# 86 products whose results nobody reads on the matrix engine, and a new hand-written order of all queues

## The chip, the cores and the metric

The kernel runs on one core of one Trainium2 chip. A core has a matrix engine (TensorE, PE in the profile), a vector engine (VectorE, DVE), a scalar engine for activations (ScalarE, ACT), GpSimd (POOL), and SyncE (SP), whose queue issues most of the DMA transfers. Each engine works through its own list of instructions in order, and they meet only through semaphores. The metric is the device time of one execution in microseconds.

## The reference

A small transformer on x of shape (8, 256, 128): four residual layers after one another, each behind a layer norm, and the first and last pair of them share the weights of the feed-forward layer.

```
x = x + attn_a(layernorm(x), Wq, Wk, Wv, Wo)      # 16 heads of 8, rotary, causal over 256 tokens
x = x + ffn(layernorm(x), w_gate, w_up, w_down)   # FP4 quantised, inner width 352
x = x + attn_b(layernorm(x), w_qkv, ln_w, w_proj) # 16 heads of 8, causal within groups of 32 tokens
x = x + ffn(layernorm(x), w_gate, w_up, w_down)

ffn:    h = silu(q(x) @ q(w_gate).T) * (q(x) @ q(w_up).T);  out = q(h) @ q(w_down).T
q(t):   per block of 16: scale = max|t| / 6, t / scale rounded to the grid 0 .5 1 1.5 2 3 4 6, times scale
attn_a: softmax(q k^T * scale + causal mask) v, then @ Wo.T
attn_b: q and k are RMS-normed with weight ln_w before the heads are split
```

## The kernel before

One batch of 256 tokens (two tiles of 128) goes through all four layers without leaving SBUF; the eight batches overlap. A batch has these stages:

- `front1`: layer norm, turn of xn to the contraction side (L788, bank 0 of `fb`), four projections for q, k and their rotated forms (L805, 128x256, fp32), rotary on DVE and POOL, and V (L810), which ACT copies to `Vf`. Q and K are split into three bf16 parts, which SP writes to DRAM (`scr_f`, L732) and reads back stacked (`Qf`, `Kf`, L741).
- `front2`: first scores. For each of 16 heads four bf16 products (L844 to L847) into bank 0 or 1 of `fb` in turn, and a maximum over each row on DVE (L1366). The maxima go back as three extra rows of `Qf` (`nmTf`, L749 on SP).
- `front3`: second scores (L875 to L878), exponential on ACT (L1089), products with V (L887, sixteen for four heads), division, projection (L902), residual.
- `ffn_a` 1 to 3: norm and quantisation; gate and up products (L981, L985); quantisation of h, turn (L997) and down projection (L1003).
- `local` 1 and 2: the attention over groups of 32, in the two banks of `lb`. Its last step, L1455, adds the result to x and raises `l_done`.
- `ffn_b` 1 to 3: the same as `ffn_a`, then the store.

`weights`, once: the FFN weights are quantised and turned (L780, L782).

The order is written out by hand in the table `TIMES`. For each engine and stage it has a line per batch with a number per step, and `weave` (below) issues the steps of an engine by rising number. A step that is early in the list waits on its semaphore and holds up what is behind it on its engine. `FFN_TURNS` says in which order the two FFNs use the two banks of `ffb`; a phase waits for the one before it.

In the first front PE issues the turn, the projections and V, and its next instruction is the first score of batch 0, which needs `Kf` read back from DRAM. At the end it works for the last batch's `ffn_b` alone, with the down projection of batch 6 just ahead.

The last two batches are finer: `SPLIT` has the quantisation of h done tile by tile. x of batches 2 to 7 is loaded by `load` on SP (L755), at the place that `TIMES["sp.load"]` gives.

Of the kernel before, what the change touches and what calls it, by code (L numbers as in the profile page):

```python
# [13 lines left out]
P = 128  # L14
NBATCH, SEQ, D = 8, 256, 128
T = SEQ // P
# [30 lines left out]

SPLIT = {("a", 6), ("a", 7), ("b", 6), ("b", 7)}
# [17 lines left out]
5 9  # L66
11 12
13 15
16 17
19 20  # L70
23 24
# [3 lines left out]
10  # L75
14
18
21
22
27  # L80
30
31""",
    "sp.load": """
0
1
2
3
4
6
7  # L90
8""",
    "sp.store": """
32
33
# [25 lines left out]
380 381 385 386 393 394 404 406 410 411 413 417 418 423 424 428 437""",  # L120
    "pe.front3": """
# [31 lines left out]
316 320 323 325 328
392 396 399 401 402
460 463 464 467 469
505 506 507 509 510""",
    "pe.ffn_b2": """
218 223 224 234 237
271 285 289 299 306
375 377 378 382 383  # L160
442 446 449 451 454
493 495 496 498 499
511 514 515 516 517
532 533 535 536 537
552 553 554 555 556""",
    "pe.ffn_a3": """
114 116 117 118
173 174 176 178
239 240 242 244
307 309 310 312  # L170
364 365 367 370
434 435 438 440
484 487 488 490
520 522 523 525""",
    "pe.ffn_b3": """
333 338 339 350
409 412 425 429
472 473 480 482
501 502 503 504
526 527 528 529  # L180
540 541 542 543
548 549 550 551
557 558 559 560""",
# [4 lines left out]
7 10 13 16  # L188
24 29 32 34
39 48 49 53  # L190
72 79 82 83
107 116 117 123
169 190 193 200
214 224 225 228""",
    "act.front2": """
6
37
69
104
# [1342 lines left out]
```

## Time and profile before

| | |
|---|---|
| median of 3 runs | 408.29 us (407.53 to 409.46) |
| profiled execution | 406.49 us, span 404.6 us |
| PE, DVE, ACT, POOL busy | 78%, 70%, 60%, 37% of the span |
| mean granted clock of TensorE | 0.884 |
| DMA | 17.56 MB, mean 43 GB/s |

A busy share is an average over stages that have different limits. The granted clock is the share of full speed that TensorE was given: it has two levels here, 1.00 (2.4 GHz) and 0.50 (1.2 GHz), and a value between them is a stretch that has both. The first low stretch that a record marks begins at 17.4 us; up to 13.9 us there is no record of the clock, and the page shows 1.00 there. Times in a timeline are from the start of the span. In the chain of waits each piece is the work that the next one waited for.

### The profile page before, as it was taken

How to read it: one execution, taken by the hardware profiler on the slowest of the kernel's cores; microseconds unless marked ns; L12 is line 12 of the kernel's file. 1: busy time of each engine (PE TensorE's matmuls, PEld its weight loads, DVE VectorE, ACT ScalarE, POOL GpSimd, SP SyncE). 2: the span in 40 equal slices, each digit the busy share in tenths (PEclk: the TensorE clock that was granted, in tenths of full speed). 3: DMA queues.
4: the chain of work that ended last, by engine and by line, in shares of the span. 5: the costliest groups of instructions: out<-in, count | busy, mean ns of one | idle time of the engine just before them, and what ended most of it. 6: DMA issues, size and time to landing. Idle time of an engine off the chain costs nothing.

```text
span 404.6 us, 9187 instructions
## 1 busy us (share of the span) xinstructions
PE 315.1 (78%) x3533; PEld 215.4 (53%) x3533; DVE 283.4 (70%) x746; ACT 241.2 (60%) x630; POOL 148.6 (37%) x210
## 2 busy tenths in 40 slices
PE   1408688698798989889798998899989676757654
PEld 0305445365565856565566676568547544535423
DVE  2626406739878899883898599879958889647551
ACT  2211173256488499587836985786898587474431
POOL 6050044131560481334256243613533556150503
PEclk9855679579999999978999999989999998989565
DMA  5570055056024000250150204000100000000000
GB/s 164 145 158 0 4 126 108 4 104 133 6 80 79 4 2 2 56 104 2 41 115 8 66 14 80 5 2 2 29 2 12 6 15 0 2 15 14 2 13 13
DMA packets 33151, 17.56 MB, mean 43 GB/s; under 512 B 1898, under 2 KB 32938, under 8 KB 33108
## 3 DMA queue, kind: packets, MB, share of 16 engines
q1 hardware_dynamic: 32820, 16.85, 18.3%
q8 instruction: 28, 0.46, 0.5%
q10 hardware_dynamic: 288, 0.13, 0.1%
q14 instruction: 15, 0.12, 0.1%
HBM read 9.43 MB, written 7.34 MB: 41 GB/s over the span
## 4 chain that ended last, share of the span: by engine, by line
PE 36%; DVE 29%; ACT 20%; issue 8%; POOL 5%; DMA 1%; SPq 1%; ACTq 0%; DVEq 0%; POOLq 0%
DVE bmax L1366 7%; PE fb L805 5%; PE fb L887 3%; PE ffb L1003 3%; PE ffb L981 3%; PE fb L844 2%; PE fb L875 2%; ACT prob L1089 2%; PE lb L944 2%; ACT Qd L1134 2%; ACT Kd L1132 2%; PE ffb L985 2%; DMA Kf<-scr_f 1%; PE lb L918 1%; PE ffb L997 1%
## 5 line engine op out<-in xcount | busy, mean ns | idle before, releaser
L1366 DVE TENSOR_REDUCE bmax<-fb 128x3 f32<-128x384 f32 x128 | 65.8, 544 | 11.1 <-PE fb L847 10.6
L1089 ACT ACTIVATE prob<-fb 128x384 f32<-128x384 f32 x128 | 59.3, 497 | 19.8 <-PE fb L878 19.4
L844 PE MATMUL fb<-Kf,Qf 50*128 50x256 bf16 x128 | 30.7, 298 | 22.4 <-DMA Kf<-scr_f 14.1
L1265 POOL TENSOR_TENSOR fa__w<-fa__w,fa__c 128x704 f32<-128x704 f32 (+1 forms) x10 | 13.8, 1378 | 56.7 <-DVE fa__w L1509 56.7
L875 PE MATMUL fb<-Qf,Kf 53*128 53x256 bf16 x128 | 29.3, 287 | 5.2 <-ACT prob L1089 4.3
L844 PEld LDWEIGHTS fb<-Kf,Qf 50*128 50x128 bf16 x128 | 10.5, 94 | 37.9 <-DVE bmax L1366 19.7
L887 PE MATMUL fb<-prob,Vf 128*32 128x128 f32 (+1 forms) x512 | 29.0, 346 | 1.3 <-ACT prob L1089 1.1
L1265 POOL TENSOR_TENSOR fb__w<-fb__w,fb__c 128x704 f32<-128x704 f32 (+1 forms) x10 | 13.7, 1374 | 43.5 <-DVE fb__w L1509 43.5
L805 PE MATMUL fb<-xnTf,wT 128*128 128x256 f32 x64 | 23.6, 533 | 2.4 <-ACT xnTf L1017 2.4
L846 PE MATMUL fb<-maskb 64*128 64x128 bf16 x128 | 24.4, 234 | 0.0
L845 PE MATMUL fb<-Kf,Qf 50*128 50x128 bf16 x128 | 24.3, 232 | 0.0
L847 PE MATMUL fb<-maskb 64*128 64x128 bf16 x128 | 24.1, 230 | 0.0
L877 PE MATMUL fb<-maskb 64*128 64x128 bf16 x128 | 23.2, 226 | 0.0
L876 PE MATMUL fb<-Qf,Kf 53*128 53x128 bf16 x128 | 23.0, 223 | 0.0
L878 PE MATMUL fb<-maskb 64*128 64x128 bf16 x128 | 22.8, 221 | 0.0
L875 PEld LDWEIGHTS fb<-Qf,Kf 53*128 53x128 bf16 x128 | 10.0, 93 | 23.6 <-ACT prob L1089 10.2
L1228 POOL TENSOR_TENSOR qk<-ra,rb 128x512 f32<-128x512 f32 x7 | 9.0, 1293 | 34.8 <-DVE rb L1347 34.8
L887 PEld LDWEIGHTS fb<-prob,Vf 128*32 128x32 f32 x512 | 14.2, 113 | 13.2 <-issue 3.2
L1003 PE MATMUL ffb<-wdT,fb__hqT 128*128 128x128 f32 (+1 forms) x96 | 16.9, 326 | 4.7 <-ACT fb__hqT L1017 4.7
L805 PEld LDWEIGHTS fb<-xnTf,wT 128*128 128x128 f32 x64 | 16.4, 269 | 7.7 <-ACT xnTf L1017 4.3
L1346 DVE TENSOR_TENSOR ra<-fb,ropet 128x512 f32<-128x512 f32 x8 | 5.5, 686 | 21.0 <-PE fb L805 20.9
L944 PEld LDWEIGHTS lb<-Kd,Qd 128*128 128x128 f32 x128 | 19.2, 215 | 0.6
(201 smaller groups left out, 942.1 us busy)
## 6 DMA issues: line engine op xcount, KB each, us to landing
scr_f<-partsf SPq DMA_DIRECT2D x16, 192.0 KB, 2.4
Qf<-scr_f SPq DMA_DIRECT2D x16, 192.0 KB, 3.8
Kf<-scr_f SPq DMA_DIRECT2D x16, 192.0 KB, 5.0
scr_f<-partsf SPq DMA_DIRECT2D x16, 128.0 KB, 1.9
xall<-in_L_attn_a_x_dram SPq DMA_DIRECT2D x8, 128.0 KB, 3.1
scr_f<-partsf SPq DMA_DIRECT2D x16, 64.0 KB, 1.6
out_dram<-xall SPq DMA_DIRECT2D x8, 128.0 KB, 1.8
ropet<-in_rope_dram SPq DMA_DIRECT2D x1, 512.0 KB, 3.6
```

Of the source, the lines that this page charges most:

```text
L805: mm = pe.matmul(fb[:, n // 2, (n % 2) * SEQ:(n % 2 + 1) * SEQ], wT[:, n, :], xnTf[:, :], start=True, stop=True)
L844: pe.matmul(S[:, 128:384], Qf[k, g, 128:256], Kf[k, g, 0:256], start=True, stop=True, skip_group_check=True)
L845: pe.matmul(S[:, 0:128], Qf[k, g, 0:128], Kf[k, g, 0:128], start=False, stop=True, skip_group_check=True)
L846: pe.matmul(ends(S, 0, 64), eye_lo[half_, :], twice(m_qk[half_, :]), start=False, stop=True, skip_group_check=True)
L847: mm = pe.matmul(ends(S, 64, 64), eye_hi[half_, :], twice(m_qk[half_, :]), start=False, stop=True, skip_group_check=True)
L875: pe.matmul(S[:, 128:384], Kf[k, g, 0:128], Qf[k, g, 0:256], start=True, stop=True, skip_group_check=True)
L887: mm = pe.matmul(S[32 * j:32 * j + 32, k * P:SEQ], Vfs[b % RING][:, k, h, :], p, start=(k == 0), stop=(k == 1), skip_group_check=True)
L944: mm = pe.matmul(lb[:, t, n * P:(n + 1) * P], Qd[:, w, :, :].rearrange("p j q -> p (j q)"), Kd[:, w, :, :].rearrange("p g k -> p (g k)"), ...
L1003: mm = pe.matmul(ffb[:, t, 0:D], w.hqT[0:k, t, c, :], wdT[0:k, c, :], start=(c == 0), stop=(c == 2))
L1089: act.activation(prob[:, slot % 8, :], S[:, 0:384], ACT.Exp).then_inc(f.s_exp, 1)
L1265: pool.tensor_tensor(w.w[:, cols], w.w[:, cols], w.c[:, cols], ALU.subtract).then_inc(w.s_hdif, t1 - t0)
L1366: dve.tensor_reduce(bmax[:, h, 1:4], fb[:, h % 2, 0:384].rearrange("p (n k) -> p n k", k=P), AX.X, ALU.max).then_inc(bmax_done, 1)
```

## The change

It adds a step function `work` to PE, with 86 matrix products in it. Each multiplies the identity by columns of the projection weights `wT` and writes a bank that nobody reads at that time: bank 0 of `lb` in the first three batches' `work`, before the local attention of batch 0 uses it or between its uses, and bank 3 of `fb` in the last, when all fronts are over. The counts are 28, 10, 8 with 256 columns and 12, 6, 22 with 128. The first product of each group waits for a semaphore: Vf of batch 0 is copied; the shifts of batch 0, and of batch 1, are turned; the last local attention is added; xq of the last batch is turned back; both halves of the last h have their gate. The others of a group wait for nothing.

Beside it, all of `TIMES` is new, for the five engines, and `FFN_TURNS` with it.

```diff
+HEAD_WORK = [28, 10, 8]
+TAIL_WORK = [12, 6, 22]
 FFN_TURNS = [
     ("a", 0, "up"), ("a", 0, "down"), ("a", 1, "up"), ("a", 1, "down"),
-    ("a", 2, "up"), ("b", 0, "up"), ("a", 2, "down"), ("a", 3, "up"),
-    ("b", 1, "up"), ("a", 3, "down"), ("a", 4, "up"), ("b", 0, "down"),
+    ("a", 2, "up"), ("b", 0, "up"), ("a", 2, "down"), ("b", 0, "down"),
+    ("a", 3, "up"), ("b", 1, "up"), ("a", 3, "down"), ("a", 4, "up"),
...
+    "pe.work": """
+3 4 5 6 7 8 9 10 11 12 13 14 15 16 17 18 19 20 21 22 23 24 25 26 27 28 29 30
+50 54 59 60 64 65 70 72 75 82
+106 111 134 139 144 148 149 155
+
+
+594 595 596 597 599 600 601 602 605 606 607 610
+612 614 615 617 619 620
+621 622 623 624 625 626 627 628 629 630 631 632 633 634 635 636 637 638 639 643 644 645""",
...
+            spare = {
+                0: (HEAD_WORK[0], 2, lb[:, 0, :], f.s_v, 1),
+                1: (HEAD_WORK[1], 2, lb[:, 0, :], f_nmT, 1),
+                2: (HEAD_WORK[2], 2, lb[:, 0, :], f_nmT, 2),
+                5: (TAIL_WORK[0], 1, fb[:, 3, :], l.s_done, NBATCH),
+                6: (TAIL_WORK[1], 1, fb[:, 3, :], ffn_b.s_xqT_ready, NBATCH),
+                7: (TAIL_WORK[2], 1, fb[:, 3, :], ffn_b.s_hg, T * NBATCH),
+            }
+
+            def work(b):
+                for n in range(spare[b][0] if b in spare else 0):
+                    yield
+                    _, width, bank, *ready = spare[b]
+                    if n == 0:
+                        pe.wait_ge(*ready)
+                    pe.matmul(bank[:, 0:width * P], identf, wT[:, 0:width, :].rearrange("p n k -> p (n k)"), start=True, stop=True)
+                yield
+
-            passes("pe", weights=weights, front1=front1, ...
+            passes("pe", work=work, weights=weights, front1=front1, ...
```

Line numbers below L46 move by 12 in the changed kernel (the projections are L817, the first scores L856, the added products L1036).

PE at the first front, before: L805 are the projections of batch 0, L810 its V, L844 to L847 the first head's scores.

```order
L805 MATMUL fb<-xnTf,wT 128x256 x4
L810 MATMUL fb<-wT,xnTf 128x128 x2
L844 MATMUL fb<-Kf,Qf 128x256
L845 MATMUL fb<-Kf,Qf 128x128
```

And now:

```order
L817 MATMUL fb<-xnTf,wT 128x256 x4
L822 MATMUL fb<-wT,xnTf 128x128 x2
L1036 MATMUL lb<-wT,identhm 128x256 x28
L856 MATMUL fb<-Kf,Qf 128x256
L857 MATMUL fb<-Kf,Qf 128x128
```

The 28 added products stand where PE had nothing between V and the first score; behind them the sixteen heads and the weights follow as before.

PE at the front of batch 1 in the changed kernel: L864 turns the shifts of batch 0, L800 turns xn, L887 is the first of the second scores.

```order
L864 MATMUL fb<-maskb,npartf 128x128 x2
L800 MATMUL fb<-identhm,xnf 128x128 x2
L1036 MATMUL lb<-wT,identhm 128x256
L817 MATMUL fb<-xnTf,wT 128x256 x4
L887 MATMUL fb<-Qf,Kf 128x256
```

One added product has come between the turn and the projections; it is so once more in the front of batch 3. Nine further ones are spread over the second scores of batch 0 and the front of batch 2.

SP before, from the end of the setup: `scr_f` are the stores of the parts, `xall` the loads of x.

```order
L755 DMA xall<-in_L_attn_a_x_dram 128x2x128 x3
L732 DMA scr_f<-partsf 128x3x256
L732 DMA scr_f<-partsf 384x1x256
L732 DMA scr_f<-partsf 128x2x256 x2
L732 DMA scr_f<-partsf 128x256 x2
L755 DMA xall<-in_L_attn_a_x_dram 128x2x128 x3
L741 DMA Qf<-scr_f 48x8x256 x2
L741 DMA Kf<-scr_f 48x8x256 x2
L749 DMA Qf<-nmTf 3x8x256 x2
```

And now:

```order
L744 DMA scr_f<-partsf 128x3x256
L744 DMA scr_f<-partsf 384x1x256
L744 DMA scr_f<-partsf 128x2x256 x2
L744 DMA scr_f<-partsf 128x256 x2
L753 DMA Qf<-scr_f 48x8x256 x2
L753 DMA Kf<-scr_f 48x8x256 x2
L761 DMA Qf<-nmTf 3x8x256 x2
L767 DMA xall<-in_L_attn_a_x_dram 128x2x128
```

All six loads of x have moved behind the first reads of Qf and Kf, and behind the shifts of batch 0, for which SP waits.

PE at the end in the changed kernel: L997 is the last up product of batch 7, L1009 turns hq, L1015 is the down projection.

```order
L1036 MATMUL fb<-wT,identhm 128x128
L997 MATMUL ffb<-wguT,fb__xqT 128x352
L1036 MATMUL fb<-wT,identhm 128x128 x21
L1009 MATMUL ffb<-identhm,fb__hq 128x128 x3
L1015 MATMUL ffb<-wdT,fb__hqT 128x128 x3
L1009 MATMUL ffb<-identhm,fb__hq 128x128 x3
L1036 MATMUL fb<-wT,identhm 128x128 x3
L1015 MATMUL ffb<-wdT,fb__hqT 128x128 x3
```

Before, the same real products stand there in the same order, with nothing between them. Earlier, eleven of the added ones stand around the down projection of batch 6, and four among the gate and up products ahead of these rows.

## Rows read from the trace of the kernel before

**Rows 1.** The page: busy time by engine, and the clock in 40 slices.

```profile
PE 315.1 (78%) x3533; PEld 215.4 (53%) x3533; DVE 283.4 (70%) x746; ACT 241.2 (60%) x630; POOL 148.6 (37%) x210
...
PEclk9855679579999999978999999989999998989565
```

**Rows 2.** Windows: stretch, its length, busy us per engine, clock, DMA share, GB/s.

```profile
17.40:48.00 30.60, 13.84 (x83) 9.39 (x84) 14.98 (x33) 5.47 (x10) 5.49 (x4) 0.50 0.30 66
...
54.90:61.70 6.80, 6.76 (x43) 4.15 (x42) 0.60 (x2) 3.56 (x8) 1.24 (x3) 0.50 0.75 155
...
72.00:85.60 13.60, 9.81 (x50) 6.00 (x49) 7.67 (x25) 3.00 (x8) 2.25 (x5) 0.50 0.32 53
...
90.00:330.00 240.00, 212.82 (x2748) 147.44 (x2747) 199.05 (x537) 176.58 (x475) 99.06 (x135) 0.98 0.17 37
...
375.70:389.40 13.70, 10.17 (x29) 6.52 (x30) 5.93 (x18) 4.41 (x10) 5.83 (x8) 0.50 0.04 11
...
392.80:404.60 11.80, 4.83 (x18) 3.74 (x18) 2.34 (x6) 2.40 (x5) 3.55 (x4) 0.50 0.04 11
```

**Rows 3.** The chain of waits: start us, us, what.

```profile
24.36 5.29 DMA Kf<-scr_f
...
30.41 1.36 PE ffb L780 x6
...
33.71 0.39 PE fb L844
...
35.08 0.39 PE fb L844
...
56.12 1.44 PE fb L887 x16
...
59.49 3.04 PE fb L805 x8
...
62.92 0.79 PE fb L887 x16
...
80.40 3.78 PE fb L805 x8
...
133.45 1.92 PE fb L805 x8
```

**Rows 4.** Windows before a fall of the clock, or without a rise.

```profile
14.00:17.30 3.30, 0.76 (x5) 0.52 (x4) 3.21 (x5) 0.45 (x2) 0.00 (x0) 1.00 0.56 172
...
33.70:41.30 7.60, 6.63 (x46) 4.45 (x47) 5.53 (x12) 0.01 (x1) 0.00 (x0) 0.50 0.00 0
...
68.60:71.90 3.30, 2.60 (x24) 1.72 (x22) 3.27 (x11) 0.38 (x1) 1.54 (x3) 1.00 0.43 120
```

**Rows 5.** Timeline of the first fronts: start, length, instruction [idle before <-releaser].

```profile
15.58 0.38 ACT L1017 ACTIVATE Vf<-fb 128x256 f32<-128x256 f32 x1 [5.37 <-PE fb L810]
...
21.32 1.46 SPq L755 DMA_DIRECT2D xall<-in_L_attn_a_x_dram  x3
...
45.65 3.17 PE L805 MATMUL fb<-xnTf,wT 128*128 128x256 f32 x8 [0.47 <-ACT xnTf L1017]
```

**Rows 6.** The end: one row of the chain, the others of the timeline.

```profile
137.84 0.86 PE ffb L1003 x6
...
376.88 0.42 DVE L1455 TENSOR_TENSOR xall<-lb,xall 128x256 f32<-128x256 f32 x1 [0.72 <-PE lb L961]
...
382.88 1.65 PE L1003 MATMUL ffb<-wdT,fb__hqT 128*128 128x128 f32 x6 [0.58 <-ACT fb__hqT L1017]
...
383.02 0.62 POOL L1257 TENSOR_TENSOR fb__xq<-fb__xw,fb__xscale 128x256 f32<-128x256 f32 x1
...
386.13 1.54 PE L981 MATMUL ffb<-wguT,fb__xqT 128*128 128x352 f32 x2 [0.47 <-ACT fb__xqT L1017]
...
396.04 0.90 PE L997 MATMUL ffb<-identhm,fb__hq 128*128 128x128 f32 x3 [5.51 <-POOL fb__hq L1272]
...
397.52 1.65 PE L1003 MATMUL ffb<-wdT,fb__hqT 128*128 128x128 f32 x6 [0.58 <-ACT fb__hqT L1017]
```

More of the change, by code:

```diff
@@ L65 @@
     "sp.front1": """
[L66 to L71, printed above, removed]
+0 1
+6 9
+10 13
+15 16
+20 21
+22 24
 25 26
@@ L74 @@
     "sp.front2": """
-10
-14
-18
-21
-22
+2
+11
+18
+19
+23
 27
 30
-31""",
+33""",
     "sp.load": """
-0
-1
-2
 3
 4
-6
+5
 7
-8""",
+8
+12
+14
+17""",
     "sp.store": """
+31
 32
-33
 34
@@ L158 @@
[L158 to L165, printed above, removed]
-    "pe.ffn_a3": """
[L167 to L174, printed above, removed]
-    "pe.ffn_b3": """
[L176 to L183, printed above, removed]
+49 51 56
@@ new lines @@
+76 79 83
+105 107 117
+165 166 170
+214 227 231
+284 290 295
+338 344 349""",
+    "pe.front2": """
[7 rows of a table added]
+416 417 422 426 427 433 436 439 440 444 447 455 459 467 468 472 477""",
+    "pe.front3": """
[7 rows of a table added]
+485 486 488 490 491 494 495 497 499 500 503 504 507 508 510 511 514 515 519 521 523 526 529""",
+    "pe.local1": """
+169 177 190
+235 241 252
+301 304 325
+390 393 403
+458 463 473
+517 520 527
+546 549 554
+574 577 579""",
+    "pe.local2": """
+199 210 216 220 224 230
+261 262 276 278 288 292
+334 341 348 351 356 358
@@ new lines @@
+410 412 419 420 424 429
+479 481 487 489 493 496
+531 534 539 540 543 544
+558 561 566 567 570 571
+582 585 590 591 592 593""",
+    "pe.ffn_a2": """
+110 114 120 124 131
+171 182 186 193 194
+240 242 243 248 249
+326 329 331 336 337
+385 391 392 396 400
+452 456 457 462 464
+509 512 513 516 518
+545 547 548 550 551""",
+    "pe.ffn_b2": """
+255 265 266 273 277
+345 352 357 362 368
+402 408 409 418 432
+482 483 484 492 498
+536 537 538 541 542
+563 564 565 568 569
+578 580 581 583 584
+609 611 613 616 618""",
+    "pe.ffn_a3": """
@@ L184 @@
+160 161 162 164
+218 219 222 225
+282 283 286 289
+373 374 377 378
+442 443 448 449
+501 502 505 506
+530 532 533 535
+557 559 560 562""",
+    "pe.ffn_b3": """
+308 313 316 320
+470 471 475 476
+522 524 525 528
+552 553 555 556
+572 573 575 576
+586 587 588 589
+598 603 604 608
+640 641 642 646""",
     "act.weights": """
@@ L253 @@
-269 280
-313 321
-359 364
-382 385
+38
+71
+105
+154
+192
+255
+299""",
+    "act.front3": """
[7 rows of a table added]
+305 306 308 309 310 313 314 316 317 318 321 323 325 326 328 330 332 334 337 340 345""",
+    "act.local1": """
+74 77 84 88 90 93
+121 126 131 134 135 139
+167 169 174 179 183 190
+231 233 238 242 243 247
+281 285 287 291 292 296
+331 335 338 342 343 346
+357 360 363 367 368 372
+382 386 387 390 391 393""",
+    "act.local2": """
+106 109 116
+144 150 162
+197 201 211
+254 256 259
+302 304 312
+351 353 358
@@ L257 @@
+376 378 381
+396 399 400""",
+    "act.ffn_a1": """
+36 37
+70 73
+114 117
+170 177
+217 224
+262 268
+307 315
+348 355""",
+    "act.ffn_a2": """
+42 45 54
+81 89 94
+129 133 136
+189 191 194
+232 237 241
+278 282 286
+327 329 333
+359 362 365""",
+    "act.ffn_b1": """
+127 132
+171 186
+225 234
+273 280
+320 324
+361 364
+385 388
 403 405""",
     "act.ffn_b2": """
-143 147 156
-195 201 206
-258 259 263
-306 308 320
-353 354 358
-372 375 378
-391 393 395
+140 145 153
+203 210 213
+245 252 258
@@ L266 @@
+301 303 311
+352 354 356
+377 379 380
+392 394 395
 407 408 409""",
     "act.ffn_a3": """
-65 68 70
+65 68 69
 103 111 112
-145 159 160
-192 209 211
-240 253 254
-286 300 301
-337 338 348 349
-373 374 379 381""",
-    "act.ffn_b3": """
-162 235 241
-255 289 292
-303 342 345
-351 362 363
-369 383 384
+143 157 158
+206 220 221
+250 271 272
+297 319 322
+336 339 347 350
+366 371 373 375""",
+    "act.ffn_b3": """
+161 180 181
+230 294 295
+300 341 344
+349 369 370
+374 383 384
 389 397 398
-400 402 404 406
+401 402 404 406
@@ L284 @@
 410 411 412 413""",
     "pool.weights": """
-1 2""",
+2 3""",
     "pool.front1": """
 0
-3 4 5 6
+1 4 5 6
 7 8 9 10
-11 14 15 16
-17 23 24 25
-26 30 32 34
-35 47 49 51
-54 60 61 64""",
+12 14 15 16
+17 23 24 26
+27 32 34 36
+40 44 47 49
+51 54 55 58""",
     "pool.local1": """
-21 27
-31 38
+21 25
+31 37
 43 48
-59 62
-68 73
-78 84
-89 95
-104 106""",
+61 63
+71 74
+80 83
+91 95
+103 105""",
     "pool.ffn_a1": """
-12 13
+11 13
 20 22
-33 36
-42 45
-55 58
-69 71
-79 82
-91 94""",
-    "pool.ffn_b1": """
@@ L315 @@
-37 39
-44 46
-57 66
-72 74
-80 83
-93 96
-103 105
-112 114""",
+30 33
+45 52
+59 60
+68 70
+76 78
+89 92""",
+    "pool.ffn_b1": """
+35 38
+50 53
+62 64
+72 73
+79 88
+93 98
+104 106
+113 114""",
     "pool.ffn_a3": """
@@ L325 @@
 28 29
-40 41
-50 53
-63 65
-75 76
-85 86 87 88
-99 100 101 102""",
-    "pool.ffn_b3": """
-52 56
-67 70
-77 81
-90 92
-97 98
+39 41
+56 57
+65 66
+75 77
+84 85 86 87
+96 97 99 100""",
+    "pool.ffn_b3": """
+42 46
+67 69
+81 82
+90 94
+101 102
 107 108
-109 110 111 113
+109 110 111 112
 115 116 117 118""",
     "dve.weights": """
-4 6 7 9 13 15""",
+4 6 7 9 13 21""",
     "dve.front1": """
@@ new lines @@
+46 49 54
+102 104 109
+167 168 171
+244 245 252
+315 318 324
+384 386 392
+441 444 453
+502 503 506""",
+    "dve.local1": """
+120 122 125 132
+175 179 182 203
+248 249 255 277
+344 346 349 363
+419 420 422 434
+483 484 487 501
+522 528 532 554
+573 575 579 597""",
+    "dve.local2": """
[7 rows of a table added]
+601 602 605 606 607 608 612 614 621""",
+    "dve.ffn_a1": """
[7 rows of a table added]
+508 510 512 513 523 525 526 530""",
+    "dve.ffn_a2": """
+79 81 84 87
+135 139 145 146
+199 200 205 207
+296 297 300 301
+355 360 361 362
+423 426 427 430
```

176 lines of the change are left out of this document (38 added, 138 removed), and 106 rows, old and new, of tables (FFN_TURNS, TIMES).

## The prediction

> **What bounds the kernel now.** I read first the page: busy shares and the slices of the granted clock [rows 1]. PE is the busiest engine (315.1 us, 78%), DVE next, and the clock of TensorE stands at about half in the first fronts and in the last batch. Then the busy time by stretch [rows 2]. From 90 to 330 us the clock is 0.98 and DVE works 199.05 of 240 us, so the middle is a matter of DVE and of the order. Outside it there are five stretches at 0.50, which is the 1.2 GHz level: 30.6 + 6.8 + 13.6 + 13.7 + 11.8 = 76.5 us. PE is busy for only part of them, so the question is how much PE work in them lies on the chain that ended last. That chain was read third [rows 3]. At the low level the four projections of a front (L805) take 3.04 and 3.78 us, at full speed 1.92.
>
> What PE did before the clock fell or stayed low [rows 4]: in 14.0 to 17.3 us it worked 0.76 us, and the clock fell. In 33.7 to 41.3 us it issued nothing but the scores of batch 0, busy for 6.63 of 7.6 us, and the clock stayed at 0.50. In 68.6 to 71.9 us, at full speed, it mostly issued scores of batch 1 (2.60 of 3.3 us) and the clock fell. The first low stretch ended at 48.0 us, when the projections of 45.65 to 48.82 us [rows 5] were nearly over. So dense fp32 products lift the clock and scores alone do not hold it. The added products are of the first kind (f32, 128x128 weights), so I take them to hold it wherever they stand close together.
>
> **The parts, against the profiled execution.** It took 406.49 us (span 404.6 and 1.9 around it), 1.8 us under the median of 408.29 that the runs show. Differences are carried over to the median.
>
> (1) 28 products, 256 columns wide, before the first scores. They begin when Vf of batch 0 is copied (15.58 + 0.38 = 15.96 us, [rows 5]), at full clock. One costs what one product of L805 costs: 1.92 / 4 = 0.48 us at full speed, 3.17 / 4 = 0.79 to 3.78 / 4 = 0.95 at half. 28 x 0.48 = 13.4, to 29.4 us. The last Kf transfer lands at 24.36 + 5.29 = 29.65 [rows 3]. They fit, with 0.3 us to spare; the last one's end is counted in each 0.48, so the room is somewhat larger.
>
> (2) First scores and turned weights. Two pairs of heads and the turns at L780 and L782, from 29.7 to about 33 us, then run at full speed. The turns stand at 1.36 us for the six of L780 [rows 3] and half as much again for L782, 2.0 us in all; half of it less the last one's latency is 0.9. The first scores give 0.4. A pair of heads repeats every 35.08 - 33.71 = 1.37 us: scores 0.39 + 3 x 0.11 and a maximum 0.57; at full speed the scores are an estimated 0.46 (half of 0.72 and 0.1 of latency), so a pair takes 1.10, and 0.27 is saved. Two such pairs: 0.5. Sum -1.8. Bounds: 0 if the clock falls at once, and -1.8 - 4 x 0.27 - 1.27 (projections of batch 1) - 0.35 (the turns ahead of them) = -4.5 if it never falls. I take -1.8, since [rows 4] show scores alone losing the clock.
>
> The page "TensorE: Matmul & The Clock Gate" of the Trainium skill (Part 4, PE-mode transpose) says that transposes do not count as PE activity in the usual way. No run here shows it alone. By it the turns at L780 would not help to hold the clock, and the sum of (2) would be nearer to -0.9.
>
> (3) One product stands between the turn of xn and the projections of batches 1 and 3. There PE waits 0.47 us for ACT before 45.65 [rows 5]. At half speed a product (0.85) reaches 0.4 past it: +0.4 each, +0.8. Bounds 0 and +1.0.
>
> (4) Nine products among the second scores of batch 0 and the projections of batch 2. 54.9 to 61.7 us is at 0.50 and PE is busy 6.76 of 6.8 us [rows 2], so here PE is the bound. Full speed saves 3.04 - 1.92 = 1.1 on L805, 1.44 - 0.79 = 0.65 on the 16 products of L887 [rows 3], and some 0.5 on the scores between: 2.3. Against this the products: of nine, three in the bound part, 3 x 0.44 = 1.3. Net -1.0. Bounds -2.3 (all in gaps) and +2.0 (nine in the chain, 4.3, less 2.3).
>
> (5) 72.0 to 85.6 us. The scores of batch 1 have no product between them; they stand one after another in the new order as before. I expect the clock to fall as it did, and 0. Bounds: -2.3 (1.9 of it L805 at 80.40) and 0. The other seven products stand among outputs of batch 1 and scores of batch 2, where the clock was full anyway; PE has gaps there: +0.2.
>
> (6) SP no longer issues three loads of x (1.46 us, [rows 5]) ahead of the reads of Qf and Kf. The reads wait for the stores' landing, so little is gained: -0.3 (bounds 0 and -1.5). The loads come later, ahead of the next reads; x of batch 2 is asked for at about 46 us, behind the shift rows of batch 0, and needed ahead of the projections at 59.49. If that cover were gone, a load of 128 KB, at most the 5.29 us of a Kf transfer, would show.
>
> (7) The end. The last local attention is added at 376.88 + 0.42 = 377.3 us; four products at the low level follow (narrow ones, half of (1): 0.40 to 0.48), to about 379.2, and may push the turn of hq behind them by about 1 us. The next turn waits for POOL anyway, so this is absorbed if the clock is up by then. After that, at full speed: down projection L1003 1.65 becomes 0.86 [rows 6], which lets batch 7's turn of xq come 1.0 earlier (bound from then on by POOL, done at 383.64). Gate products L981: 1.54 becomes about half, and the second gives about 0.35: 1.1. At the very end a turn of 0.90 and two down projections of 1.65 on the chain become an estimated 0.45, 0.86 and 0.86: 2.0. The 21 products ahead of it need 21 x 0.24 = 5.0 us, and PE sits idle 5.5 us before 396.04. The three between the last turn and last product cover ACT's copy and stick out an estimated 0.2; the four before the first down projection 0.2. Sum -1.0 - 1.1 - 2.0 + 0.4 = -3.7. Bounds: -5.0 and, if all is at half speed, 19 x 0.48 = 9.1 against 5.5: +3.6, and 1 above.
>
> (8) The new order of all engines. From 90 to 330 us DVE idles 41 us. A new order can only move within these: a tenth of it is 4 us either way. On DVE the last batch's first FFN is finished 11 instructions earlier of 649. One takes 283.4 / 746 = 0.38 us, so 4.2 us, but what is pushed behind it must still be done; I count a quarter, -1.0. Bounds -4 and +4.
>
> Sum: -1.8 + 0.8 - 1.0 + 0.2 - 0.3 - 3.7 - 1.0 = -6.8. 406.49 - 6.8 = 399.7; from the median 401.5.
>
> **The rivals.** About 0.5% (2 us) is what a measurement of this kernel can tell from no change.
>
> A, the clock holds through the first scores too, and on into the front of batch 3: another 2.7 from (2), 2.3 from (5) and the 0.8 of (3) back, less 0.4 for lost cover: 396.1. For it: 28 products right ahead, and earlier transfers. Against: [rows 4].
>
> B, the head's gain is eaten before 90 us by DVE and ACT, and the order gives nothing. Then only the end counts, -3.7: 404.6. For it: in 72.0 to 85.6 us PE is busy for only 9.81 of 13.6 us [rows 2], so part of what it does faster ends in waiting. Against: from 55 to 61.7 us PE has no gap. The same page (Part 1, the tip on the warm-up budget) puts the cost of the clock's ramp at under 1% of a typical span; by that rule all of it here would be below 4.0 us, a time of 404.3 or more. The trace speaks against it: 76.5 us at half clock are 19% of the span, though only a part of them lies on the chain.
>
> C, the new order loses in the middle. The order of all five queues changes, and turns of the two FFNs change place. If it costs the 4 us of (8) and head and end bring 4: 408.
>
> D, slower: the added products run at half speed. This is decided at 16 us. Each of the 28 at half speed takes 0.32 to 0.47 us more; from the second on they are later than Kf. All 28 at 0.85: 15.96 + 23.8 = 39.8 against 29.7, +10.1, and the end adds 3.6 at most; with 0.8 for (3) and without gains elsewhere 408.3 + 10.1 = 418 or more; if the clock comes back after some ten of them, +3.5, the end's +1 and no gain: 413. For it: the 0.76 us of work from 14.0 to 17.3 did not hold the clock. Against: it is up at 15.96, and from then on there is no gap.
>
> **Chances.** Forecast 0.45 (own range 398.5 to 404.5), A 0.20, B 0.13, C 0.11, D 0.07, more than A 0.04. Faster by over 0.5% (below 406.3) is forecast, A, B and the rest: 0.82, less 0.02 for their edges: 0.80. C lies half within and half beyond: same 0.10, slower 0.10. The range leaves out D, half of C and what lies beyond A: 394.5 to 407.0.
>
> **What would show it.** (1): the first scores start at 29.3 to 30.0 us; a start at 31 or later speaks for D. (2): the turns of L780 take 0.7 us, and the low clock returns before 37. (4): no low clock between 52 and 64. (5): low clock again from about 70 to 82; if not, A. (7): clock 1.00 from about 380 (old time) to the end, the last down projection 0.86 us long. (8): last batch's first FFN done earlier than the head's gain alone explains. Wrong would be the whole if the clock's level did not change where the products stand, or if the first scores came late.

## The result, and the profile after

The changed kernel took 398.43 us (median of 4 runs, 395.03 to 401.78), the one before 408.88 us beside it: a ratio of 0.971, 95% interval 0.966 to 0.976. The forecast was 401.5 us, range 394.5 to 407.0. The profiled execution took 399.24 us, with a span of 397.3 us. A ratio here is taken from the executions of a kernel that lie within 1.5% of its fastest, a median from all of them, so the two can differ, and of the kept traces e1's (409.45 us) and e8's (456.2 us at a mean clock of 0.651) are not of such executions. Behind the added products the line numbers of the changed kernel are 32 above those of before (L1403 is now L1435).

The page of the kernel after (the rows that answer [rows 1]):

```profile
PE 335.2 (84%) x3705; PEld 240.6 (61%) x3705; DVE 283.4 (71%) x746; ACT 243.3 (61%) x630; POOL 150.6 (38%) x210
...
PEclk9996699599999699899999999999999988986799
```

PE has 20.1 us more work, DVE has exactly what it had. The clock row is full in the first slices and in the last ones. Windows of the kernel after: stretch, its length, busy us of PE, PEld, DVE, ACT and POOL, granted clock, DMA share, GB/s. They answer [rows 2] and [rows 4].

```profile
13.20:33.50 20.30, 17.33 (x104) 13.73 (x102) 14.65 (x24) 5.26 (x9) 5.59 (x4) 1.00 0.42 92
33.70:47.10 13.40, 10.45 (x54) 6.93 (x54) 5.90 (x15) 0.76 (x2) 0.00 (x0) 0.50 0.04 12
47.30:71.00 23.70, 21.58 (x218) 14.11 (x217) 10.04 (x30) 12.31 (x28) 7.21 (x8) 1.00 0.42 95
71.20:81.30 10.10, 6.07 (x29) 4.19 (x28) 6.36 (x21) 2.38 (x6) 3.77 (x7) 0.50 0.25 70
90.00:330.00 240.00, 214.87 (x2748) 151.33 (x2747) 200.59 (x544) 179.91 (x481) 98.49 (x133) 0.97 0.16 36
354.60:364.60 10.00, 8.46 (x24) 5.32 (x23) 3.99 (x7) 5.64 (x15) 3.21 (x3) 0.50 0.00 0
371.60:378.20 6.60, 5.76 (x27) 5.46 (x27) 4.81 (x15) 3.82 (x9) 4.59 (x6) 0.50 0.00 0
378.40:395.30 16.90, 14.55 (x104) 12.45 (x102) 6.94 (x18) 4.96 (x10) 4.89 (x6) 1.00 0.03 9
```

Of the five low stretches of [rows 2] the first is 13.4 us long in place of 30.6, the second is gone, the third 10.1 in place of 13.6, the fourth 6.6 in place of 13.7, and the fifth gone: from 378.4 us to the end the clock is full. The clock first falls among the first scores of batch 0, 5.7 us after the dense products ended. The middle is at 0.97, as good as before. But there is a new low stretch, 10.0 us long, ahead of the last local attention, at 354.6 us; before, the clock was low there for 3.2 us only, from 362.2.

The chain of waits after (start us, us, what), which answers [rows 3]:

```profile
23.52 5.29 DMA Kf<-scr_f
...
29.32 0.76 PE ffb L792 x6
...
42.40 0.85 PE lb L1036 x2
43.26 3.41 PE fb L817 x8
...
78.76 0.85 PE lb L1036 x2
79.62 2.67 PE fb L817 x8
...
393.90 0.86 PE ffb L1015 x6
```

The turns at L792 (L780 before) take 0.76 us in place of 1.36, so the clock was full at 29.3. The added products at 42.40 and 78.76 are on the chain, at half speed, as step (3) has them. Timeline of PE after, first fronts and end (answers [rows 5] and [rows 6]):

```profile
15.62 12.35 PE L1036 MATMUL lb<-wT,identhm 128*128 128x256 f32 x56 [0.47 <-ACT Vf L1049]
...
43.05 3.62 PE L817 MATMUL fb<-xnTf,wT 128*128 128x256 f32 x8
...
59.25 1.99 PE L817 MATMUL fb<-xnTf,wT 128*128 128x256 f32 x8
...
79.41 2.87 PE L817 MATMUL fb<-xnTf,wT 128*128 128x256 f32 x8
...
373.20 2.08 PE L1036 MATMUL fb<-wT,identhm 128*128 128x128 f32 x8 [0.84 <-DVE xall L1487]
...
381.90 0.86 PE L993 MATMUL ffb<-wguT,fb__xqT 128*128 128x352 f32 x2 [0.25 <-ACT fb__xqT L1049]
...
385.38 4.96 PE L1036 MATMUL fb<-wT,identhm 128*128 128x128 f32 x42
390.84 0.55 PE L1009 MATMUL ffb<-identhm,fb__hq 128*128 128x128 f32 x3 [0.50 <-POOL fb__hq L1304]
```

The 28 products (56 records, since an fp32 product shows as two) took 12.35 us, 0.44 each, and were done at 27.97, ahead of Kf's landing at 28.81. At the end 21 products fill PE up to the turn of hq (5.51 us of idle time in [rows 6], 0.50 now), and that turn takes 0.55 us in place of 0.90.

Three places serve below as milestones of the way: where DVE adds the first front's result, the last front's, and the last local attention's. DVE after:

```profile
69.37 0.42 DVE L1435 TENSOR_TENSOR xall<-fb,xall 128x256 f32<-128x256 f32 x1
...
305.98 0.42 DVE L1435 TENSOR_TENSOR xall<-fb,xall 128x256 f32<-128x256 f32 x1
...
372.74 0.42 DVE L1487 TENSOR_TENSOR xall<-lb,xall 128x256 f32<-128x256 f32 x1
```

And before, of which the third stands in [rows 6], at 376.88:

```profile
72.36 0.41 DVE L1403 TENSOR_TENSOR xall<-fb,xall 128x256 f32<-128x256 f32 x1
...
317.15 0.41 DVE L1403 TENSOR_TENSOR xall<-fb,xall 128x256 f32<-128x256 f32 x1
```

The first front ends 3.0 us earlier, the last one 11.2, the last local attention only 4.1. The rest, 3.2 us, comes behind it.

### The profile page after: what moved, and what is told of

The parts are those of the page before. It is cut to its first block, busy times and chain, and to the rows that moved or that the text cites. A ratio compares the mean times of both kernels' runs of the same rounds, so it can differ in the third digit from the quotient of the medians.

```text
span 397.3 us, 9531 instructions
## 1 busy us (share of the span) xinstructions
PE 335.2 (84%) x3705; PEld 240.6 (61%) x3705; DVE 283.4 (71%) x746; ACT 243.3 (61%) x630; POOL 150.6 (38%) x210
## 4 chain that ended last, share of the span: by engine, by line
PE 39%; DVE 25%; ACT 15%; issue 11%; POOL 5%; DMA 4%; SPq 1%; DVEq 0%; POOLq 0%; ACTq 0%
DVE bmax L1398 5%; PE ffb L1015 4%; PE fb L899 3%; PE fb L856 3%; PE ffb L993 3%; DMA Kf<-scr_f 3%; PE ffb L997 2%; PE fb L817 2%; PE fb L887 2%; ACT prob L1121 2%; PE lb L1036 2%; PE ffb L1009 2%; PE lb L956 2%; PE fb L906 1%; DVE nmaxl L1466 1%
## 5 line engine op out<-in xcount | busy, mean ns | idle before, releaser
L1398 DVE TENSOR_REDUCE bmax<-fb 128x3 f32<-128x384 f32 x128 | 66.2, 547 | 14.3 <-PE fb L859 14.0
L856 PE MATMUL fb<-Kf,Qf 50*128 50x256 bf16 x128 | 30.8, 290 | 6.2 <-DVE bmax L1398 4.6
L899 PE MATMUL fb<-prob,Vf 128*32 128x128 f32 (+1 forms) x512 | 28.1, 338 | 1.6 <-ACT prob L1121 1.5
L887 PE MATMUL fb<-Qf,Kf 53*128 53x256 bf16 x128 | 28.5, 280 | 1.2 <-ACT prob L1121 0.7
L1036 PE MATMUL lb<-wT,identhm 128*128 128x256 f32 x92 | 24.8, 405 | 0.5 <-ACT Vf L1049 0.5
L858 PE MATMUL fb<-maskb 64*128 64x128 bf16 x128 | 24.5, 227 | 0.0
L859 PE MATMUL fb<-maskb 64*128 64x128 bf16 x128 | 24.1, 223 | 0.0
L856 PEld LDWEIGHTS fb<-Kf,Qf 50*128 50x128 bf16 x128 | 10.7, 93 | 21.1 <-DVE bmax L1398 14.3
L889 PE MATMUL fb<-maskb 64*128 64x128 bf16 x128 | 22.5, 219 | 0.0
L890 PE MATMUL fb<-maskb 64*128 64x128 bf16 x128 | 22.1, 215 | 0.0
L887 PEld LDWEIGHTS fb<-Qf,Kf 53*128 53x128 bf16 x128 | 10.0, 93 | 19.2 <-issue 10.7
L899 PEld LDWEIGHTS fb<-prob,Vf 128*32 128x32 f32 x512 | 14.0, 110 | 12.0 <-ACT prob L1121 3.1
L817 PE MATMUL fb<-xnTf,wT 128*128 128x256 f32 x64 | 19.7, 463 | 1.0 <-ACT xnTf L1049 1.0
L956 PE MATMUL lb<-Kd,Qd 128*128 128x128 f32 x128 | 19.5, 302 | 0.0
```

What stands on the lines that cost most here:

```text
L817: mm = pe.matmul(fb[:, n // 2, (n % 2) * SEQ:(n % 2 + 1) * SEQ], wT[:, n, :], xnTf[:, :], start=True, stop=True)
L856: pe.matmul(S[:, 128:384], Qf[k, g, 128:256], Kf[k, g, 0:256], start=True, stop=True, skip_group_check=True)
L858: pe.matmul(ends(S, 0, 64), eye_lo[half_, :], twice(m_qk[half_, :]), start=False, stop=True, skip_group_check=True)
L859: mm = pe.matmul(ends(S, 64, 64), eye_hi[half_, :], twice(m_qk[half_, :]), start=False, stop=True, skip_group_check=True)
L887: pe.matmul(S[:, 128:384], Kf[k, g, 0:128], Qf[k, g, 0:256], start=True, stop=True, skip_group_check=True)
L899: mm = pe.matmul(S[32 * j:32 * j + 32, k * P:SEQ], Vfs[b % RING][:, k, h, :], p, start=(k == 0), stop=(k == 1), skip_group_check=True)
```

## The experiments

All times stand beside runs of the kernel before on the same chip. Executions of one kernel scatter by several us (before: 406.4 to 411.7 but for three; e1: 402.9 to 410.6), so sizes are taken from the ratios (in us of 409) and the medians, and places from the traces.

**Order, head and tail apart.** Four kernels that differ only in two lines:

```diff
 e1  HEAD_WORK = [0, 0, 0]     TAIL_WORK = [0, 0, 0]
 e2  HEAD_WORK = [28, 10, 8]   TAIL_WORK = [0, 0, 0]
 e3  HEAD_WORK = [0, 0, 0]     TAIL_WORK = [12, 6, 22]
 e4  the changed kernel again
```

> The new order with none of the 86 products. Theory 1 (the recorded forecast): the order is worth 1 us and the products 5.8, so this run comes about 1 us under the kernel before, ratio 0.998. Theory 2, from the two traces: the head's gain of 3.0 us at the end of front 0 is gone at the end of front 2 (140.8 after, 140.6 before), the last front ends 11.2 us earlier and the last local attention 4.1 us earlier, which is the order's work; the tail behind it is 3.2 us shorter, which is the products' work. Then this run keeps about 4 of the profiled 7.3 us: ratio 0.985 to 0.992. Theory 3, all comes from the products: ratio 1.000 or above. In the trace the clock is low from about 17 to 48 us and from 378 to the end.

> The new order with the 46 products of the first fronts and none at the end. Theory 1: 2.1 us under e1 (ratio lower by 0.005). Theory 2: the first fronts end 3 us earlier than in e1 but DVE-bound work from 90 us on swallows it, so within 1 us of e1. Clock full from 14 to about 33 us and in 47 to 68 us, low at the end as in e1.

> The new order with the 40 products at the end and none in the first fronts. Theories 1 and 2 agree: 3.5 us (0.009) under e1, since nothing behind the last local attention can swallow it. A rival, that the products at the end only delay PE and the clock there came from elsewhere: equal to or above e1. Clock full from about 378 us to the end.

> The changed kernel itself beside the other three on the same chip: ratio 0.966 to 0.976 as measured before. If head and tail add up (e2 and e3 against e1), it is e1 less both differences; by theory 2 it is equal to e3 within 1 us.

| kernel | median us (before: 408.52) | ratio to before | 95% interval | us of 409 | us by medians |
|---|---|---|---|---|---|
| e1, order alone | 407.99 | 0.9948 | 0.9910 to 0.9985 | -2.1 | -0.5 |
| e2, order and head | 404.21 | 0.9888 | 0.9851 to 0.9925 | -4.6 | -4.3 |
| e3, order and tail | 403.33 | 0.9872 | 0.9831 to 0.9913 | -5.2 | -5.2 |
| e4, all | 399.25 | 0.9770 | 0.9732 to 0.9807 | -9.4 | -9.3 |

The order gives 2.1 us by the ratio and 0.5 by the median of all twelve executions, so it is small and its size is open between the two. The head's products give 2.5 us (3.8 by medians) without the tail's and 4.2 (4.1) with them, the tail's 3.1 (4.7) without the head's and 4.8 (5.0) with them. The parts add up to 7.7 of 9.4 us by ratios and to 9.0 of 9.3 by medians; the rest is within the four intervals, so no interaction of head and tail is shown. That the order did nearly all of it and the head's gain was lost is out: the head's products pay in both pairs.

How they pay is in the trace of e3. Its milestones:

```profile
75.62 0.42 DVE L1435 TENSOR_TENSOR xall<-fb,xall 128x256 f32<-128x256 f32 x1
...
309.67 0.42 DVE L1435 TENSOR_TENSOR xall<-fb,xall 128x256 f32<-128x256 f32 x1
...
379.31 0.42 DVE L1487 TENSOR_TENSOR xall<-lb,xall 128x256 f32<-128x256 f32 x1
```

And PE's projections of batches 1 and 2 in e3:

```profile
45.21 3.78 PE L817 MATMUL fb<-xnTf,wT 128*128 128x256 f32 x8 [0.47 <-ACT xnTf L1049]
...
64.29 3.50 PE L817 MATMUL fb<-xnTf,wT 128*128 128x256 f32 x8
```

Without the head's products the new order is late in the head: batch 2's projections start at 64.29 us, before they did at 59.42 (the timeline of the kernel before), and the first front ends 3.3 us later than before (2.1 in e1's trace, 74.45 against 72.36). Two things stand behind it in e3. The new order has put more of PE's work ahead of these projections (56 records of products with V from batch 1's projections on, where 32 stood), and PE does it at half speed: the sixteens of L899 take 1.51 us each from 53.94 to 62.85, while before one of the two (L887) ran at full clock, in 0.86. (The page of e3 shows 1.00 up to 77 us because its first record of the clock is later; the durations tell the level.) With the products they start at 59.25, 5.0 us earlier than in e3.

From the first front's end to the last one's the new order then needs 234.1 us (e3) or 236.6 (after), against 244.8 before; from there to the last local attention it needs 69.6 and 66.8 against 59.7. So it wins 8 to 11 us up to the last front, gives back 7 to 10 of them behind it, where the other work now stands, and a small gain is left. Part of what is given back is the clock: in e10 below, where it is full from 334.2 to 392 us, the last stretch takes 63.2 us, 3.6 less than after. No run tells how the rest is made up.

**The same products in the old order.** The old tables, and the 86 products put behind the same real products of PE:

```diff
+    "pe.work": """
+2.01 ... 2.28
+21.01 24.01 28.01 ...
```

> The 86 products in the order of before: each stands behind the same real instruction of PE as in the changed kernel, the other engines are untouched. Theory 1 (products and order are two edits that add up: order 2 us, products 7): ratio 0.982 to 0.986. Rival, that the new order was needed for the products to pay (they hold up PE in an order that was not made for them): ratio 0.990 or above. A second rival, that the order alone lost something in the first fronts which the products hide: lower than the changed kernel, under 0.977.

Ratio 0.9925 (0.9896 to 0.9953), 405.83 us. The products give 3.1 us in the old order (3.6 by medians); in the new one they give 0.977 against 0.9948, 7.3 us (8.7 by medians). That is the rival of the expectation, 0.990 or above: in the old order the products do not pay as well. Milestones of e5:

```profile
69.81 0.42 DVE L1433 TENSOR_TENSOR xall<-fb,xall 128x256 f32<-128x256 f32 x1
...
317.77 0.41 DVE L1433 TENSOR_TENSOR xall<-fb,xall 128x256 f32<-128x256 f32 x1
...
377.46 0.43 DVE L1485 TENSOR_TENSOR xall<-lb,xall 128x256 f32<-128x256 f32 x1 [0.67 <-PE lb L973]
```

The first front ends 2.6 us earlier than before, the last 0.6 later: here the head's gain is lost. It is gone by the third front's end (140.00 us, 140.15 before). Two things of the products stand in that stretch: one on the chain at half speed, as the chain of e5 shows,

```profile
77.51 0.85 PE lb L1034 x2
78.36 2.34 PE fb L817 x8
```

and the other seven of batch 1's group, some 0.44 us each. From 85.7 to 95.0 us PE is busy for 9.30 of 9.3 us, before and in e5, at full clock, so a product there is paid in full. That these two are the whole loss is argued, not shown: no run took the seven away alone, and e12 below has the same seven and loses nothing there.

**Is it that PE is occupied, or how much of the array works?** The same 86 products, each on 32 rows and 32 columns of weights:

```diff
-pe.matmul(bank[:, 0:width * P], identf, wT[:, 0:width, :]...)
+pe.matmul(bank[0:32, 0:width * P], identf[0:32, 0:32], wT[0:32, 0:width, :]...)
```

> The changed kernel with each added product cut to 32 rows and 32 columns of weights (it streams as many columns of the moving operand, so PE is as busy by the profile). This tells 'PE was kept occupied' from 'the clock was kept up by full products'. If occupation is what holds the clock, it is as the changed kernel, ratio 0.97 to 0.98. If the clock follows how much of the array works, it falls at about 17 us, the 28 products run at half speed and take 0.85 us each, the first scores start at 36 to 40 us instead of 29.3, the tail's 21 also come late by some 4 us: ratio 1.01 to 1.03, slower than the kernel before.

Ratio 1.0609 (1.0546 to 1.0672), 434.29 us: 25 us slower than before, and well beyond the 1.01 to 1.03 that was expected even for this side. PE in e6, the 28 products and the first scores:

```profile
16.54 24.09 PE L1036 MATMUL lb<-wT,identhm 32*32 32x256 f32 x56 [0.47 <-ACT Vf L1049]
...
40.57 0.40 PE L856 MATMUL fb<-Kf,Qf 50*128 50x256 bf16 x2
```

Its last 33 us, as a window:

```profile
400.00:433.00 33.00, 29.60 (x107) 19.05 (x107) 7.60 (x20) 5.00 (x11) 4.88 (x6) 0.50 0.03 8
```

The 28 small products ran one behind another for 24.09 us, 0.86 us each, which is what a full one takes at the low level (0.85 at 42.40). (The page of e6 shows 1.00 there, since its first record of the clock is later; the durations tell the level. At 117.15 us, where the clock is recorded as full, one small product takes 0.61 us, against 1.05 at 61.34.) At the end PE is busy for 29.60 of 33 us and the clock stays at 0.50. The fair partner is e9 below, whose 28 full products begin at the same moment and also at half speed (the V products ahead of them, at 14.84 us, take 1.22 us in e9 and 1.23 in e6, 0.71 after):

```profile
16.54 13.79 PE L1045 MATMUL lb<-wT,identhm 128*128 128x256 f32 x56 [0.47 <-ACT Vf L1073]
30.26 0.29 PE L865 MATMUL fb<-Kf,Qf 50*128 50x256 bf16 x2
```

By the length, 13.79 us in place of 12.35, some three or four of them ran at half speed (an estimate from 0.85 and 0.44 us a product) and the others at full. So with PE equally occupied, the clock came up where the whole array worked, and did not where a sixteenth of it did. Whether rows, columns or something else of the product decides is open. e6 is also what rival D would have looked like: the first scores came at 40.57, the forecast for D had 39.8. The Trainium skill ("TensorE: Matmul & The Clock Gate", Part 1, what's actually happening) says that the clock follows how busy PE has been. The trace of e6 does not agree (24.09 us without a gap, and 0.86 us a product to the last), unless a small product counts for little.

**More products.** Six narrow ones between the heads of batch 0's first scores, three wide ones behind them and eight wide ones among and behind the first scores of batch 1 (e7), twelve wide ones around the last batch's local attention (e8), and both (e9):

```diff
+    "pe.fill": """
+35.5 37.5 39.5 41.5 43.5 45.5
+47.5 47.6 47.7 91.5 94.5 97.5 99.5 101.5 103.5 103.6 103.7
+577.1 577.2 577.3 577.4 577.5 577.6 578.5 591.5 591.6 592.5 593.1 593.2
```

> The changed kernel with 17 more products where its clock still fell: six of 128 columns behind pairs of the first scores of batch 0, three of 256 behind its last scores, eight of 256 among and behind the first scores of batch 1. Theory (scores alone lose the clock, 33.6 to 47.2 and 71.1 to 81.4 us): the clock stays at 1.00 from 14 to beyond 100 us, a pair of heads in batch 0 takes 1.10 instead of 1.37 us, the projections of batch 1 1.9 instead of 3.4: front 0 ends 3 us earlier, and 2 to 4 us of it are left at the end: ratio 0.967 to 0.973. Rival: each product delays a score on the chain by 0.2 to 0.4 us and the clock's gain is used up: no change against the changed kernel (0.977).

> The changed kernel with 12 more products of 256 columns around the last local attention (six behind its projections, one before the turn of q and k, five behind its outputs), where the clock was low at 354.4 to 364.7 and 371.5 to 378.3 us. Theory: the clock stays at 1.00 from 338 us to the end; gate, up, local scores and down projections in between run at full speed, 2 to 3 us earlier at the end: ratio 0.969 to 0.973. Rival: these stretches wait for ACT, DVE and POOL in turn, so faster products end in waiting: within 0.5 us of the changed kernel.

> The changed kernel with the 17 products of e7 and the 12 of e8 together: 115 in all. If both gains add (0.977 to 0.965 and to 0.970): ratio 0.955 to 0.961, which would beat the changed kernel. If the stretch at the end is set by something else once the head is faster: as e7, 0.965. Clock at 1.00 from 14 us to the end but for the stretches between 310 and 345 us.

| kernel | median us (before) | ratio to before | 95% interval |
|---|---|---|---|
| e7, 17 more in the head | 394.23 (409.44) | 0.9652 | 0.9604 to 0.9700 |
| e8, 12 more in the tail | 395.77 (409.44) | 0.9697 | 0.9649 to 0.9746 |
| e9, both | 393.40 (409.46) | 0.9599 | 0.9560 to 0.9637 |

Against e4, e7 gains 4.8 us, e8 3.0, e9 7.0. The interval of e8 overlaps that of e4 a little, so its gain is likely rather than certain; e7 is a little better than either side of its expectation. A window of e7:

```profile
14.00:131.00 117.00, 106.96 (x988) 74.03 (x987) 75.80 (x191) 56.34 (x136) 33.24 (x40) 1.00 0.30 63
```

And of e9:

```profile
14.00:110.00 96.00, 88.63 (x714) 61.74 (x714) 59.12 (x149) 38.02 (x86) 27.53 (x32) 0.96 0.37 77
345.00:392.00 47.00, 37.41 (x346) 29.65 (x344) 26.12 (x66) 21.71 (x55) 16.58 (x20) 0.96 0.04 12
```

In the trace of e7 there is no low stretch in the first fronts at all. In the trace of e9, which has the same products there, the clock is at 0.50 from 36.6 to 43.2 us, with PE busy for all of these 6.6 us; behind that it is full to 110 us and beyond. The first scores' chain with its products between, in e7:

```profile
34.93 0.42 PE lb L1060 x2
35.34 0.21 PE fb L865
...
36.03 0.42 PE lb L1060 x2
36.45 0.21 PE fb L865
...
37.29 0.42 PE lb L1060 x2
37.71 0.21 PE fb L865
```

A pair of heads repeats every 1.11 and 1.26 us, product included, against 1.37 in [rows 3] without one at half clock. The first score of a pair takes 0.21 in place of 0.39. So at full clock a product there pays for itself on the chain. e9, at 393.4 us, is the best kernel of this study; it beats e8 by more than the intervals, and e7 by less.

**What the first 28 are worth, and more products in the old order.**

```diff
 e10  e9 with  HEAD_WORK = [0, 10, 8]
 e11  e1 with  HEAD_WORK = [28, 0, 0]
 e12  e9's 115 products in the old tables
```

> As e9, without the 28 products ahead of the first scores. It tells whether these 28 matter once products stand among the first scores. If they only warm the first 4 us of the scores, the run loses my term for them, 1.8 us (0.004) against e9, and the clock comes up within one or two pairs of heads. If a low clock once entered is not left by scores with one product of 128 columns per pair, the whole of batch 0's scores and the projections behind run at half speed and it loses 4 to 5 us (0.011).

> The new order with the first 28 products and no others. By my terms they are worth 1.8 us against e1 (ratio 0.990), and the 10 and 8 behind them the rest of the 2.4 that e2 showed. Rival: the low clock at 53 to 66 us, which only the 10 prevent, is the dearer part: equal to e1, 0.995.

> All 115 products of e9 in the order of before, each behind the same real instruction of PE. e5 showed front 0 ending 2.6 us earlier and nothing of it left at 140 us in the old order. If the old order swallows whatever the head gains, only the end's 12 come on top of e5: ratio 0.985. If it was only that e5's clock gain was small, the head's other 4 us come through too: 0.974 or below.

e11: 406.39 us, ratio 0.9914 (0.9882 to 0.9946), 1.4 us below e1 (2.5 by medians), with intervals that overlap. e10: 394.88 us, 0.9659 (0.9618 to 0.9700), 2.5 us above e9 (1.5 by medians), overlapping too. So the 28 products are worth some 1.4 to 2.5 us, near to the 1.8 of step (2), but neither pair alone tells it from nothing. In e10 the clock stays low through all of batch 0's first scores, to 43.8 us, and still it loses less than the 4 to 5 us that were expected for that case.

e12: 402.84 us, 0.9807 (0.9762 to 0.9851), between the two sides of its expectation. In the old order the 115 products give 7.9 us, in the new one 14.3 (0.9599 against 0.9948). In e12's trace the first front ends at 69.27 us, the third at 137.48 and the last at 314.38, each some 3 us earlier than before; at the last local attention (376.51) 0.4 of it are left. So here the head's gain is lost behind the last front. Turned round, this is what the order is worth once the clock is up: e9 and e12, measured side by side at a mean clock of 0.97, have the same 115 products and lie 9.4 us apart (8.5 by the ratios), where e1 and the kernel before lie 0.5 to 2.1 apart.

## Why the prediction was right, and what in it was not

**(1) right in this trace, and with some luck.** The 28 products took 0.44 us each where 0.48 was counted, full clock from the first on. The first scores started at 28.86 (the timeline of after), right behind Kf and half a microsecond ahead of the forecast's 29.3. The products ran at full clock in e2, e5 and e12 too. But in e4, which is the same kernel, and in e7, e9 and e11 the products began at 16.5 us at half speed, took 13.5 to 15.0 us and were done after Kf had landed: the first scores started at 30.24, 31.43, 30.26 and 29.96 us, later than the 29.69 of before. These four lost 0.3 to 1.7 us where (1) had none; the premise "at full clock" at 15.96 us holds in half of the traces. The bound of half speed is what e6 shows.

**(2) right.** The low clock came back at 33.7 us, the turns took 0.76 us (0.7 forecast), and the 28 alone bring 1.4 to 2.5 us (1.8). By the rule on transposes that stands there (the Trainium skill, "TensorE: Matmul & The Clock Gate", Part 4) it would have been 0.9, below both of these, but no run tells the turns apart.

**(3) right.** Both products stand on the chain with 0.85 us each, between the turn and the projections. From the start of the turn to that of the projections it takes 1.52 us after and 1.13 before in batch 1 (44.52 to 45.65), 1.55 and 1.14 in batch 3: 0.4 each, as forecast.

**(4) right in kind, mis-sized; (8) within what can be told.** There is no low clock from 47.3 to 71.0, as said. (8) had -1.0 for the order, and e1 has -2.1 by the ratio and -0.5 by the median. But it is not one sum spread over the middle, as (8) had it. In the head the order costs 2.1 us (e1) to 3.3 (e3, first front's end at 75.62 against 72.36), and behind that it gains. And (4) was priced against the old order, -1.0 for the bound part from 54.9 to 61.7 us. The products and the full clock take the head's cost of the new order away again: from batch 1's projections to batch 2's the way is 19.08 us in e3 and 16.20 after, 2.9 us less where step (4) had 1.0. Up to the first front's end they bring 6.2 us against e3 (5.1 against e1), 3.0 against before. The forecast for all of the head was 1.8 ((2) to (5); 2.1 with the loads). The part that survives to the end is 2.5 to 4.2 us. This is where most of the missing 2.6 us (6.8 forecast, 9.4 in e4) went: 86 products that were counted at 5.8 us in all bring 7.3 to 8.7 in the new order, and 3.1 to 3.6 in the old one, against which they were priced. The ratio beside the recorded result, 0.971, makes the change 11.8 us; by it more is missing, and no run says where.

**(5) right as to the clock.** Low from 71.1 to 81.4, where 70 to 82 was said. Its other term, +0.2 for seven products where PE has gaps, is doubtful: in the old order PE had no gap from 85.7 to 95.0, and e5 lost its head gain behind 78 us (e12 did not).

**(6) right as far as it can be seen.** Kf is on its way at 23.52 in place of 24.36 and lands 0.8 us earlier, and the first scores, which wait for it, start 0.8 earlier; 0.3 was counted. In e5 and e12, with the loads in their old place, Kf is on its way at 24.37 and 24.38; in e1, e2, e3 and e10, with the loads moved, at 23.55 to 23.92. In e4, e7, e9 and e11 nothing comes of it, since PE is the later one.

**(7) right in size: -3.7, measured -3.1 (e3 against e1) and -4.8 (e4 against e2).** In the trace, from the last local attention's add to the end of the span: 27.7 us before, 24.6 after. The three terms, from [rows 6] and the rows above. The gate product of batch 7 starts 9.25 us behind that add before and 9.16 after, so 0.1 gained where 1.0 was forecast. The first products there ran at the low level (8 records in 2.08 us at 373.20, 0.52 each product) and the clock was full only from 378.4, so they pushed the turns behind them by about what the faster down projection gave back. In e4, the same kernel, the clock is full from 364.4 us on, and with its add at 372.77 the gate product starts 8.08 us behind it:

```profile
364.40:396.00 31.60, 23.37 (x225) 19.77 (x222) 18.37 (x48) 11.50 (x25) 9.48 (x12) 1.00 0.05 14
...
380.85 0.86 PE L993 MATMUL ffb<-wguT,fb__xqT 128*128 128x352 f32 x2 [0.25 <-ACT fb__xqT L1049]
```

It is 8.1 too in e7, e9, e10 and e12, where the clock is full there, and 9.1 to 9.3 in e3 and e5, where it is not. So this term is 0 to 1.2 us by the level at which the clock stands when the last local attention ends, and (7), which took it to be low there and the 1.0 to come all the same, had that link wrong. The gates then give 1.0 (8.90 us from 386.13 to POOL's start on hq at 395.03; 7.94 now, from 381.90 to 389.84), 1.1 forecast. The very end gives 2.1 (404.6 - 395.03 = 9.57; 397.3 - 389.84 = 7.46), 2.0 less 0.2 forecast. The bound for half speed was too low: it counts 19 products where the text has 21, and in e6 the way from that add (394.91 us) to the end is 38.4 us, 10.7 more than before, where the bound allowed 4.6.

**The rivals.** A did not come, but its size was right: e7 is what it describes, the clock held through the first scores and into batch 3's front, and it stands 4.8 us below e4, where A was put 5.4 below the forecast. B had the head's gain eaten. With the old order that happens (e5 by the third front, e12 behind the last one); with the new one it does not. The rule named with B, a ramp of under 1% of the span (the Trainium skill, the same page, Part 1, the tip on the warm-up budget), does not cover this kernel, whose clock stands low in five stretches: the products alone bring 7.3 us of 409 in e4 and 14.3 in e9, which is 1.8% and 3.5%. C had a mechanism that is real and a sign that is wrong: the order costs in the head and gains behind it. D was decided at the 28 products, as it said, but not as a yes or no: in e4, e7, e9 and e11 they began at half speed and some three to six ran so before the clock rose. Where it did not rise, in e6, D's price was too low: 434 us against "418 or more".

## What to carry to other kernels

Where a profile shows long stretches at half clock with PE's work on the chain, products that nobody reads, put in PE's waits, can pay (1.8 to 3.5% here). Place them so that they end before the next operand lands, and count some of them at half speed (in four of eight traces the 28 overran by 0.3 to 1.7 us). Place them between short scores too, where at full clock one of 0.42 us costs less than the half clock does. Price a new order and such products together: the new order here is worth 0.5 to 2.1 us alone and 8.5 to 9.4 once the clock is up, and a product among work that already fills PE is paid in full.

## What the runs showed of the hardware that was not expected

Not whether PE is occupied but how much of its array works decided the clock in this place: 28 products of 32 x 32 in an unbroken 24.09 us stayed at 0.86 us each (e6), while of 28 of 128 x 128 that began at the same moment and the same low level (e9) all but the first few ran at full speed. The first scores, on 50 rows, kept PE busy for 6.63 of 7.6 us before [rows 4] and did not raise the clock either. With six narrow products of 128 x 128 among them a full clock held in one trace (e7) and was lost in two: at 36.6 us in e9, with the same products in the same order, and at 38.4 in e12. They did not raise a low one: in e10, where nothing dense runs ahead, the same mix stood at half, as its windows show.

```profile
34.00:38.00 4.00, 4.00 (x25) 2.74 (x26) 2.86 (x7) 0.00 (x0) 0.00 (x0) 0.50 0.00 0
38.00:41.00 3.00, 3.00 (x20) 2.03 (x16) 2.04 (x4) 0.00 (x0) 0.00 (x0) 0.50 0.02 5
...
43.00:44.00 1.00, 1.00 (x4) 0.72 (x3) 0.86 (x5) 0.00 (x0) 0.00 (x0) 0.54 0.00 0
```

From 34 to 41 us PE has no gap at all, and the clock is 0.50. It rose just before 44, in a row of wide products that began at 41.70 us (e10's timeline); in e9 too it rose only there, at 43.2. So what six products among the scores do to the clock is not settled here. What the times show is that e10 and e9 are 1.5 to 2.5 us apart, and both well below e4.

The clock is also not the same in every execution of one kernel. In the two traces of the changed kernel it stood at half when the added products began (e4) and at full (after), and in the last stretch it was full from 364.4 us (e4) and low from 371.6 to 378.2 (after). That moved the first scores by 1.4 us (28.86 against 30.24) and the last gate product by 1.1 (9.16 against 8.08 behind the last add). A term read from one trace at such a place is no surer than that.
